# Third layer's attention: the first half of the value products ahead of the score on TensorE, and VectorE's value copy ahead of its block turn

## What is computed

```python
def _cross_attention(q_in, kv_in, wq, bq, wk, bk, wv, bv, wo, bo, bias_k, bias_v):
    qh = (q_in @ wq + bq).reshape(b, q_len, H, K)          # H = 16 heads of K = 128
    kh = (kv_in @ wk + bk).reshape(b, t, H, K)
    vh = (kv_in @ wv + bv).reshape(b, t, H, K)
    kh = jnp.concatenate([kh, jnp.broadcast_to(bias_k, (b, 1, H, K))], axis=1)
    vh = jnp.concatenate([vh, jnp.broadcast_to(bias_v, (b, 1, H, K))], axis=1)
    logits = jnp.einsum('bqhk,bthk->bhqt', qh, kh) / scale
    weights = jax.nn.softmax(logits, axis=-1)
    ctx = jnp.einsum('bhqt,bthk->bqhk', weights, vh).reshape(b, q_len, H * K)
    return ctx @ wo + bo

h = _layer_norm(x, ln1_scale, ln1_offset)
x = res + _cross_attention(h, xf_1, ...)
h = _layer_norm(x, ln2_scale, ln2_offset)
x = res + _cross_attention(h, xf_2, ...)
```

## Time and profile before

| | us |
|---|---|
| median of 3 runs | 2236.97 (2236.34 to 2238.52) |
| the profiled execution | 2238.51 |
| its span, first to last instruction | 2236.5 |
| first and last score of the third layer's attention | 706.56 and 1700.12 |
| busy over the span: TensorE, VectorE, ScalarE, GpSimd | 94%, 66%, 57%, 29% |

### The profile page before, as it was taken

How to read it: one execution, slowest core, us unless ns; L and a number is a source line. 1 busy time by engine, 2 the same in 40 slices (tenths; PEclk the granted TensorE clock), 3 DMA queues, 4 the chain that set the end, 5 groups by cost and what they waited for, 6 DMA issues and landing times. The chain is left out here.

```text
span 2236.5 us, 47492 instructions
## 1 busy us (share of the span) xinstructions
PE 2106.0 (94%) x17700; PEld 1734.0 (78%) x17700; DVE 1473.7 (66%) x2828; ACT 1282.1 (57%) x3304; POOL 646.0 (29%) x661
## 2 busy tenths in 40 slices
PE   6999979999897999999999999999998999999899
PEld 4666656888696888888888888888887877776688
DVE  5888854555454766666667666666675349999963
ACT  4777754566643554444445544444455448988853
POOL 4444321111134412030304212030101137677711
PEclk8999999999999999999999999999998999999999
DMA  4000020000102223232322223222223020000000
GB/s 137 16 16 12 2 57 2 2 2 2 39 1 95 90 76 106 73 102 81 105 79 91 87 80 104 80 96 69 69 67 131 21 59 2 2 2 2 2 10 29
DMA packets 119007, 117.16 MB, mean 52 GB/s; under 512 B 6656, under 2 KB 91136, under 8 KB 117760
## 3 DMA queue, kind: packets, MB, share of 16 engines
q1 hardware_dynamic: 118784, 114.13, 15.9%
HBM read 78.72 MB, written 35.39 MB: 51 GB/s over the span
## 5 line engine op out<-in xcount | busy, mean ns | idle before, releaser
L866 ACT ACTIVATE l_probs<-l_s_psum,l_neg_max 128x129 f32<-128x129 f32 x512 | 182.8, 364 | 254.7 <-DVE l_neg_max L948 254.7
L972 DVE TENSOR_TENSOR x<-x,l_o_psum 128x512 f32<-128x512 f32 x256 | 176.0, 688 | 95.5 <-PE l_o_psum L823 95.4
L953 DVE SCALAR_TENSOR_TENSOR l_context_low<-l_c_psum,cols,l_context_high 128x512 fp32r<-128x512 f32 x128 | 95.9, 749 | 181.9 <-ACT l_context_high L861 181.7
L1504 DVE TENSOR_REDUCE l_neg_max<-l_psum 128x2 f32<-128x512 f32 x256 | 163.3, 683 | 46.8 <-PE l_psum L1294 46.4
L691 POOL TENSOR_TENSOR l_head_w_high<-l_head_raw,one 128x768 fp32r<-128x768 f32 x30 | 44.4, 1481 | 511.1 <-PE l_o_psum L823 465.7
L2575 POOL TENSOR_TENSOR l_probs<-l_probs,l_mask_add 128x512 f32<-128x512 f32 x128 | 162.0, 1288 | 76.6 <-DVE l_probs L2803 76.6
L854 ACT ACTIVATE l_KT<-l_k_psum,cols 128x512 f32<-128x512 f32 x128 | 88.1, 688 | 165.8 <-PE l_k_psum L114 165.8
L1433 ACT ACTIVATE l_PT<-l_psum 128x512 f32<-128x512 f32 x256 | 132.2, 603 | 54.9 <-PE l_psum L1322 54.9
L2745 ACT ACTIVATE l_probs<-l_probs,l_neg_max 128x128 f32<-128x128 f32 x512 | 159.8, 396 | 5.4 <-DVE l_neg_max L2810 5.1
L783 PE MATMUL l_s_psum<-l_KT,l_QT 128*128 128x129 f32 x1024 | 144.6, 283 | 17.1 <-issue 1.6
L783 PEld LDWEIGHTS l_s_psum<-l_KT,l_QT 128*128 128x128 f32 x1024 | 123.9, 190 | 39.8 <-issue 38.5
(11 more groups left out here) (321 smaller groups left out, 6215.6 us busy)
## 6 DMA issues: line engine op xcount, KB each, us to landing
l_moving<-l_turned SPq DMA_DIRECT2D x127, 256.0 KB, 2.0
l_PT<-l_moving SPq DMA_DIRECT2D x508, 64.0 KB
l_head_raw<-in_l_heads SPq DMA_DIRECT2D x32, 384.0 KB, 4.4
l_w<-in_l_w SPq DMA_DIRECT2D x4, 1024.0 KB, 9.8
l_ctx_in<-in_ctx_T SPq DMA_DIRECT2D x16, 256.0 KB, 5.8
l_value_raw<-in_l_values SPq DMA_DIRECT2D x8, 512.0 KB, 4.8
l_value_rows<-in_l_rows SPq DMA_DIRECT2D x8, 512.0 KB, 6.0
l_x_in<-in_x_T SPq DMA_DIRECT2D x16, 128.0 KB, 2.2
```

The source lines that it names most:

```text
L866: last = act.activation(probs[:, i, :], scores[:, i // 2, i % 2, :], ACT.Exp, bias=neg_max[:, i:i + 1], scale=1.0, accum_out=den[:, i:i + 1])
L953: dve.scalar_tensor_tensor(out=context[1][:, :], in0=c_bank[:, :], scalar=vector("bias_v", s), in1=context[0][:, :].bitcast(F32), op0=ALU. ...
L972: dve.tensor_tensor(out=x, in0=x, in1=o_bank[:, :], op=ALU.add).then_inc(o_free, 1)
L1504: dve.tensor_reduce(neg_max[:, u % 2, qt, at:at + 2], bank[:, :].rearrange("p (e k) -> p e k", e=2), AX, ALU.max, negate=True).then_inc(fr ...
```

## The change

Two entries of the list of `order2` move within iteration p. value_a of p+3 goes ahead of score of p, where it had been behind it. values_kept of p+2 goes ahead of moved of p-1, where it had been behind it. No instruction is added or removed, and ScalarE, GpSimd and SyncE have the same order as before.

```diff
         step("share", 1)
         step("out_a", 3)
+        if 0 < p and p + 2 < STEPS2:
+            steps.append(("values_kept", (p + 2) // 4, (p + 2) % 4))
         step("moved", 1)
         steps.extend(("heads_next", j) for j in range(2 * H) if heads_at[j] == p)
         steps.extend(("values_next", n) for n in range(8) if values_at[n] == p)
         steps.extend(("rows_next", n) for n in range(2, 8) if 16 * n - 18 == p)
-        if 0 < p and p + 2 < STEPS2:
-            steps.append(("values_kept", (p + 2) // 4, (p + 2) % 4))
         steps.extend([("normed", 10, 1)] if p == STEPS2 else [])
         if p:
             step("key", 0)
         step("out_b", 3)
         steps.extend([("turn", LAST2)] if p == STEPS2 else [])
+        if p + 3 < STEPS2:
+            steps.append(("value_a", (p + 3) // 4, (p + 3) % 4))
         step("score", 0)
         steps.extend(("scaled", n) for n, at in norm_at.items() if at + (n == 1) == p - 1)
-        if p + 3 < STEPS2:
-            steps.append(("value_a", (p + 3) // 4, (p + 3) % 4))
         step("probs_a", 0)
         step("context", 2)
         step("probs_b", 0)
```

## The result

The changed kernel takes 2210.95 us (median of 4 runs, 2209.59 to 2216.53) against 2236.81 for the kernel before: a ratio of 0.9886, with a 95% interval of 0.9873 to 0.99. So 25.9 us are gained by the medians where 42.6 were forecast, and the time is 2 us above the upper end of the range. The profiled execution took 2209.59, its span 2207.7 against 2236.5. That is 28.8 us less: the execution profiled before was the longest of its four, and the one profiled now is the shortest of its four. What follows accounts for these 28.8. Measured again in two later sets of runs, the same kernel gave 0.9848 (0.9833 to 0.9864) and 0.9865 (0.9849 to 0.9881). The gain is certain, and its size moves by some 0.4% between sets. What moves it is part of what follows.

The account below looks back on a forecast made before the run. TensorE bounds the stage, its score waiting for ScalarE's KT: 119 steps x 0.40 = 47.6, less 3 for stretched shares, 1.5 for late transfers and 0.5 for a norm step, gives 42.6, so 2194.4 us; range 2185 to 2209.

Parts of the forecast that it names:

- late transfers: Context on TensorE waiting for transposed probabilities as cover shrinks from 11.0 to 9.4: 1.5 us allowed.
- one norm step: One step in which the norm's scaling holds VectorE: 0.5 us allowed.
- stretched shares, seven roundings: VectorE's share taking 2.09 instead of 0.69 beside GpSimd's value roundings: 3 us allowed, 0 to 8 possible.
- The step of 7.34: TensorE's quiet step after the change, 0.40 shorter, with 0.87 from score to context.
- a bare wait: Rival: only the score's wait goes, nothing at the seams; 0.31 a step, so 2205; chance 0.14.
- a saved seam: Rival: score to context takes 0.80, the seam saved whole; 0.47 a step, so 2186; chance 0.10.
- KT's spare: ScalarE's KT is ready before TensorE wants the score's weights, with 0.2 left after 0.07 of signalling.
- VectorE's loop: Loop through score, exponents, context, share, addition and out_b: 7.15 without slack, 0.19 to spare, so TensorE stays the bound.
- The swap: VectorE's values_kept ahead of the block turn: earns nothing itself, but without it value_a is 0.34 late each step.
- a rival in which *every* way is 11.0: Rival: transposed probabilities come late at context, a step takes 8.15, kernel slower at 2287; chance 0.03.
- the first rival: Only TensorE's wait goes, order saves nothing at the seams; 2205, chance 0.14; rows 4 and 5 held against it.
- the rival "given back at VectorE": Saved wait lost to stretched shares or a VectorE loop some 0.3 longer; 2199 to 2212, chance 0.14.

Follow-up runs that it names:

- the products alone: Changed kernel with values_kept back behind moved, so the kernel before with only value_a ahead of the score: 2225.8 us, ratio 0.9938.
- the second paced kernel: Changed kernel with large loads halved or spread, value roundings held, and four of the start's loads behind the first transfers: 2206.13 us, ratio 0.9855.
- the changed kernel again: The changed kernel unaltered, measured once more beside its variants on one chip: 2203.5 us against 2237.27 for the kernel before.
- halved loads: Changed kernel with 512 KB loads of value weights and rows cut into two of 256 KB, those of weights two iterations later: 2201.91 us, ratio 0.9842.
- held roundings: Changed kernel with GpSimd's value roundings from group 2 on and head 20's waiting for VectorE's share to end: 2211.16 us, ratio 0.9882.

## Why the prediction was wrong in size

Against the prediction's own sum, span for span, 13.8 us are missing (16.7 by the medians). In its terms:

| term | forecast | measured |
|---|---|---|
| quiet steps | 119 x 0.40 = 47.6 | 116 x 0.362 = 42.0 |
| late transfers | 1.5 | 7.8 |
| one norm step | 0.5 | 2.6 (two steps) |
| stretched shares, seven roundings | 3 | 2.1 |
| step 64, steps 0 to 2, first score, behind the last | 0 | 0.7 |

- **What bounds it: right.** KT's wait was the loss, and it is gone. In the products alone, where only value_a moves, KT's wait is gone too.
- **The step of 7.34: right in kind, 0.03 too small.** Every distance holds but one. value_a to the score is 0.70, out_b 0.70, and score to context 0.90, not the 0.87 that I had worked out between bounds of 0.80 and 0.96. Over the stage this term is 5.6 us short, the second largest part of what is missing: the gain is 0.362 and not 0.40, and it comes in 116 steps and not 119. The rivals of a bare wait (0.31 a step) and of a saved seam (0.47) are both out, since the quiet step gained 0.37.
- **KT's spare: right.** Forecast 0.2 on top of the 0.07 of signalling, and 0.28 is there between KT's end and the load of the weights.
- **VectorE's loop: right in kind, and looser than I had it.** The share comes at 4.17, the addition at 4.78 and the copy at 5.37, where I had 4.31, 4.92 and 5.53. TensorE is never late for it in a quiet step.
- **The swap: right.** It earns nothing alone, and the products rest on it. Its price was over-sized, 0.34 forecast and 0.20 measured: VectorE was 0.15 earlier than I had it, and I left out the 0.08 of cold start.
- **The stretched shares: a little under the allowance.** Two of seven met the share fully (2.43 and 2.40 beside GpSimd's 1.89 and 1.90). In both GpSimd had started first, by 0.01 and 0.06 us. Where the share started 0.39 and 0.24 ahead, at 857.16 and 1098.58, it took 0.98 and 0.83, and GpSimd's instruction 2.35 and 2.34. I wrote that the share ends with GpSimd's instruction. In rows 7 and here it ends 0.55 behind it. In the changed kernel again it was step 34 (8.58), with step 50 at 8.13.

```profile
975.19 1.89 POOL L703 TENSOR_TENSOR l_value_w_high<-l_value_raw,one 128x1024 fp32r<-128x1024 f32 x1
975.20 2.43 DVE L978 TENSOR_TENSOR l_probs<-l_probs,l_rden 128x512 f32<-128x512 f32 x1
...
978.38 0.35 PE L819 MATMUL l_o_psum<-l_head_w_high,l_context_high 128*128 128x256 f32 x1 [1.22 <-DVE x L972]
```

- **The late transfers, 1.5 forecast and 7.8 measured: this is the step that failed.** I had seen the mechanism and the cover shrink from 11.0 to 9.4 (it is 9.67: turn 5.97 behind its score, context 0.90 behind the score two steps on). I wrote that the rows bound the ways by 11.0 and do not show that they fit into 9.4, and then put the danger into a rival in which *every* way is 11.0, with 0.03, and 1.5 us into the sum. The true case lay between: most ways fit, and some of those behind a large load don't. The kernel before had the list to read it from, since 4 of its transfers took over 3.5 us and 16 over 2.5, against a median of 2.0. Their cover had room for them. I priced the one wait that showed and not the ones that the cover hid.
- **The norm step: right in place, sized too small.** I had 0.5 for it, and steps 66 and 70 lost 2.6. The kernel before already had a stall of 1.47 in step 66, which its long scaling on VectorE explains.
- **A stall is not worth its length: missing altogether.** Of the 7.8 and the 2.6, three times 1.6 us is the clock. Step 2 of the kernel before had it already, with a stall of 2.28 and a mean clock of 0.86, and the prediction leaves it out.
- **Against the first rival I claimed too much.** I set 0.79 against 0.70 "for the same three matmuls" by rows 4 and 5. Those rows have the 0.79 only; the 0.70 was half of the six key matmuls. The rows of the changed kernel have it. That the kind of operand makes the difference is not shown, since place and operand change together.

The range ended at 2209, and the first result was 2210.95; the other two medians, 2203.5 and 2208.03, are inside. The forecast of 2194.4 is below all three, so the miss is the sum's and not that of one set. The three times lie where the rival "given back at VectorE" (2199 to 2212) had put them, but not for its reason: VectorE's loop was looser than forecast and the stretched shares cost 2.1 of an allowed 3. That two medians fall into the range is luck of that kind.

What stays open: why a transfer issued at the same distance behind the same load takes 4.85 us in one execution and 3.48 in another, and what besides its length decides whether a stall loses the clock. Nothing was run on these.

## What to carry to other kernels

When a change shortens a loop that is bound by one engine, list every transfer and every slow helper whose cover the loop is, and compare its longest time, not its median, with the new cover: what never waited before is what will wait after. Where the traces show the clock falling behind stalls of 2 us or so, price such a stall at nearly twice its length, and don't count on it either way. Spread the large loads before the latency-bound transfers need the queue, and move with a late load everything that stands behind its users on any engine.

## What the runs showed of the hardware

- **The clock after a stall.** All stalls of 1.2 to 1.89 us in the stages of the fourteen traces kept the granted clock at 1.00. All longer than 2.65 lost it, up to one of 8.29: TensorE worked at 0.50 behind them. Between 1.98 and 2.65 there were 12 that lost it (1.98, 2.08, 2.20, 2.24, 2.28, 2.40, 2.46, 2.54, 2.56, 2.59, 2.64, 2.65) and 5 kept it: 2.08 and 2.29 (steps 4 and 9 of the second paced kernel), 2.15 (step 0 of the changed kernel again), 2.21 (step 66 with the products alone) and 2.64 (step 66 with halved loads). So 2.08 and 2.64 stand on both sides, and the length alone does not decide there; what else does was not tested. The one of 1.98 came 7.7 us behind one of 1.79. In steps 8, 48 and 66 of the changed kernel, and behind the stall of 2.08, the clock was low for 3.4 us, and the step lost 1.8 to 1.9 us beyond the stall. After the start's wait of step 2 it was low for 6.8 us with halved loads and with held roundings, and from within the stall of 8.19 on for 10.2.
- **The order of matmuls has a price of its own.** The score with the context behind it takes 0.90, with a value matmul behind it 0.80; the same three value matmuls take 0.79 behind the score and 0.70 behind out_b. A score, or three value matmuls, that had to wait is 0.08 to 0.09 slower to the next group.
- **One load in front of a short transfer.** A transfer of 256 KB that takes 2.0 us took up to 4.85 when issued 3 us behind a load of 512 KB, and 5.27 behind one of 384 KB that was issued 0.44 ahead. Others at 3 us behind such a load took from 2.6 to 4.4. With no two loads in an iteration, transfers over 3.5 us fell from 5 to 8 in a trace to 2.
- **An issue that waits holds what is queued behind it.** SyncE's issues run in the order of the list. With the roundings held, the transfer of step 68 was issued 2.20 us behind its turn, behind a load that waited for GpSimd, and TensorE stood 4.16.
